# Norms of both graph layers tile by tile on VectorE, two residual products inside the attention loop, and the first expert block's tokens fetched ahead of the block table

## The reference, cut to what matters

```
h0  = layernorm(x)
h   = gat(h0; W1, 4 heads x 256) + b1          # layer 1, 1024 columns
h   = relu(layer_norm(h) * g1 + be1) + (h0 @ Wr1 + br1)
h1  = h
h   = gat(h1; W2, 1 head x 768) + b2           # layer 2
h   = layer_norm(h) * g2 + be2 + (h1 @ Wr2 + br2)
x   = x + h
y   = layernorm(x)                             # then the block's own norm, twice in a row
y   = y + causal_attention(norm(y))            # 12 heads
sel = argmax(norm(y) @ Wg)                     # one expert for each token
x   = x + y + relu(norm(y) @ W1[sel] + b1) @ W2[sel] + b2
```

## Time and profile before

| | us |
|---|---|
| median of 3 runs | 1133.53 (1133.08 to 1135.2) |
| the profiled execution | 1131.86 |
| its span, first to last instruction | 1129.8 |
| TensorE busy in it | 1042.2 (92%) |
| VectorE busy | 747.1 (66%) |
| ScalarE busy | 561.1 (50%) |
| GpSimd busy | 192.2 (17%) |

### The profile page before, as it was taken

One profiled execution on the slowest core, in us unless ns is written; L12 is line 12 of the kernel. 1 busy time (PEld: TensorE's weight loads), 2 busy tenths in 40 slices (PEclk: granted clock), 3 DMA queues, 4 the chain that ended last, 5 costly groups with the idle time before them and its releaser, 6 DMA issues.

```text
span 1129.8 us, 19057 instructions
## 1 busy us (share of the span) xinstructions
PE 1042.2 (92%) x6176; PEld 651.9 (58%) x6177; DVE 747.1 (66%) x1327; ACT 561.1 (50%) x744; POOL 192.2 (17%) x182
## 2 busy tenths in 40 slices
PE   5999888998999799989989399999999999999997
PEld 3555557745776576566768245555555555555554
DVE  6667768796665674259976598941118898989511
ACT  2667655702250253158853377731117777877311
POOL 2000000075205531045001111100101120301000
PEclk9999999999999899989999599999999999999999
DMA  8300030003507400030014599960007999999200
GB/s 307 101 0 0 1 112 1 1 18 133 127 1 152 84 1 1 1 108 2 3 60 130 174 384 332 387 237 18 24 0 258 384 358 372 372 369 383 96 17 3
DMA packets 92263, 155.60 MB, mean 138 GB/s; under 512 B 36507, under 2 KB 36587, under 8 KB 92214
## 3 DMA queue, kind: packets, MB, share of 16 engines
q1 hardware_dynamic: 89814, 149.20, 38.4%
q0 software_dynamic: 2400, 5.77, 1.4%
HBM read 153.21 MB, written 7.77 MB: 142 GB/s over the span
## 4 chain that ended last, share of the span: by engine, by line
PE 74%; DVE 13%; issue 5%; DMA 3%; ACT 2%; POOL 1%; DVEq 1%; SPq 0%; ACTq 0%; POOLq 0%
PE psum L1433 31%; PE psum L1669 17%; PE psum L1644 15%; DMA low<-in_L_ffn_W_dram 2%; PE psum L1421 2%; DVE area L1302 2%; PE psum L1471 2%; PE psum L1653 2%; PE psum L1565 1%; DVE smalls L975 1%; DVE area L987 1%; PE psum L1640 1%; DVE area L1057 1%; DVE area L1273 1%; DVE area L1134 1%
## 5 line engine op out<-in xcount | busy, mean ns | idle before, releaser
L1302 DVE TENSOR_TENSOR area<-low,area 128x1536 f16<-128x1536 f32 x144 | 245.8, 1754 | 14.0 <-ACT area L924 13.8
L1433 PE MATMUL psum<-area,low 128*125 128x512 f16 (+4 forms) x1116 | 245.9, 381 | 5.8 <-DVE low L1155 3.2
L1644 PE MATMUL psum<-area,low 128*128 128x512 f16 x972 | 220.4, 381 | 0.0
L924 ACT ACTIVATE area<-low 128x1536 f16<-128x1536 f32 x138 | 200.6, 1484 | 37.1 <-DMA low<-in_L_ffn_W_dram 30.8
L1669 PE MATMUL psum<-area,low 128*128 128x384 f16 x1296 | 219.0, 327 | 0.0
L1433 PE MATMUL psum<-area 125*128 125x64 f16 (+10 forms) x1452 | 195.8, 289 | 8.2 <-DVE area L1273 4.8
L1433 PEld LDWEIGHTS psum<-area,low 128*125 128x125 f16 (+2 forms) x1116 | 143.2, 141 | 101.6 <-issue 59.2
L1669 PEld LDWEIGHTS psum<-area,low 128*128 128x128 f16 x1296 | 127.1, 98 | 80.6 <-issue 1.3
L1433 PEld LDWEIGHTS psum<-area 125*128 125x128 f16 (+3 forms) x1452 | 126.9, 122 | 60.3 <-DVE area L1273 12.2
L1644 PEld LDWEIGHTS psum<-area,low 128*128 128x128 f16 x972 | 95.3, 98 | 113.6 <-issue 2.5
L935 ACT ACTIVATE low<-psum 128x512 f32<-128x512 f32 x54 | 31.9, 591 | 158.4 <-PE psum L1644 152.0
(11 more groups left out here) (226 smaller groups left out, 1205.4 us busy)
## 6 DMA issues: line engine op xcount, KB each, us to landing
low<-in_L_ffn_W_dram SPq DMA_DIRECT2D x144, 768.0 KB, 8.3
area<-in_L_gnn_W_dram SPq DMA_DIRECT2D x2, 3072.0 KB, 12.0
area<-in_L_gnn_Wr_dram SPq DMA_DIRECT2D x2, 3072.0 KB, 15.6
low<-in_x_dram SPq DMA_DIRECT2D x10, 336.0 KB
area<-in_L_ffn_Wv_dram SPq DMA_DIRECT2D x6, 384.0 KB, 6.2
area<-in_L_ffn_Wq_dram SPq DMA_DIRECT2D x6, 384.0 KB, 7.2
area<-in_L_ffn_Wk_dram SPq DMA_DIRECT2D x6, 384.0 KB, 6.5
area<-in_L_ffn_Wp_dram SPq DMA_DIRECT2D x2, 1152.0 KB, 6.7
```

The costliest lines, as they stand in the source:

```text
L924: act.activation(unit_parts(u)[0], raw_view(u), ACT.Copy).then_inc(high_ok, 1)
L1302: dve.tensor_tensor(low_, raw_view(u), high_, ALU.subtract).then_inc(low_ok, 1)
L1433: ins = pe.matmul(place(name)[0:parts, at:at + w], left(q), right(q)[:, at:at + w], start=(q == 0), stop=(q == k - 1))
L1644: ins = pe.matmul(psum[:, (c % 2) * BANK:(c % 2 + 1) * BANK], ht[x_][:, k, :], w1_s[c][w_][:, k, :], start=False, stop=(k == KD - 1 and x_ ...
```

## The change

*Layer 1.* The norm starts inside the loop's last head. Behind the evacuation of tile t (`behind1`) VectorE takes its statistics, then `centred` computes (row - mean) * g1 in one pass, and `shifted1` of the tile before computes rstd * row + be1. GpSimd keeps only the inverse roots, one per tile. The residual products of tiles 1 and 2 are taken as four halves of 512 columns at TensorE's steps 8, 15, 17 and 19, copied out of PSUM by ScalarE; tiles 3 and 4 stay behind the loop. VectorE's order there: residual rows 0 to 2, low half of W2, joins 0 to 2, then row and join of tiles 3 and 4.

*Layer 2.* The tile is centred and scaled by g2 in `behind2`; the factor rstd goes into the pass that adds it to the sum. GpSimd adds be2+br2 to x (`shift_x`), and each tile's load of x has a semaphore of its own. `residual_sum(0)` lies behind the statistics of tile 3, `first_norm_twice(0)` and `residual_sum(1)` behind those of tile 4.

*Routing.* Block 0 always belongs to expert 0, so its tokens follow from the ranks alone: an own item `ids0`, made before the block table; GpSimd fetches from it directly; ScalarE applies scale and shift for this block. TensorE turns these tokens before it makes `ids`.

```diff
+RES1_HALVES = {8: (1, 0), 15: (1, 1), 17: (2, 0), 19: (2, 1)}
...
+            def centred(rows_, t, g):
+                dve.wait_ge(var_ok, norms[0])
+                return dve.scalar_tensor_tensor(out=rows_[:, t, :], in0=rows_[:, t, :], scalar=mv[:, t, 0:1], in1=g,
+                                                op0=ALU.subtract, op1=ALU.mult)
...
-            graph_attention(1, HEADS, HID, agg1, row1["b1"])
-            variance(agg1, HC)
-            for t in range(T):
-                normal(agg1[:, t, :], agg1[:, t, :], t).then_inc(epi_a, 1)
+            def shifted1(t):
+                dve.wait_ge(rstd_ok, rows_normed + t + 1)
+                return dve.scalar_tensor_tensor(out=agg1[:, t, :], in0=agg1[:, t, :], scalar=rstd[:, t:t + 1],
+                                                in1=row1["be1"], op0=ALU.mult, op1=ALU.add)
+            def behind1(t):
+                was_emptied(dve, ("agg", 1, (HEADS - 1) * T + t))
+                moments(agg1, HC, t, t + 1)
+                centred(agg1, t, row1["g1"]).then_inc(epi_a, 1)
+                if t >= 1:
+                    dve.wait_ge(epi_a, t)
+                    shifted1(t - 1).then_inc(epi_b, 1)
+            graph_attention(1, HEADS, HID, agg1, row1["b1"], behind1)
+            dve.wait_ge(epi_a, T)
+            shifted1(T - 1).then_inc(epi_b, 1)
...
+            for t in range(3):
+                residual_row(t)
+            graph_low(1, w2_parts)
+            for t in range(3):
+                join_residual(t)
+            for t in range(3, T):
+                residual_row(t)
+                join_residual(t)
...
+                    if layer == 1 and i in RES1_HALVES:
+                        by_x0_half(*RES1_HALVES[i])
...
+            def behind2(t):
+                was_emptied(dve, ("agg", 2, t))
+                moments(agg2, D, t, t + 1)
+                centred(agg2, t, row2["g2"]).then_inc(epi_a, 1)
+                if t == T - 2:
+                    residual_sum(0)
+                if t == T - 1:
+                    first_norm_twice(0)
+                    residual_sum(1)
...
+            def shift_x(t):
+                pool.wait_ge(x2_in[t], 32)
+                pool.tensor_tensor(total[:, t, :], total[:, t, :], row2["be2"], ALU.add).then_inc(epi_b, 1)
+            for t in range(T):
+                if t == T - 1:
+                    inverse_root_twice(0)
+                inverse_root(t, t + 1)
+                if 1 <= t <= 3:
+                    shift_x(t - 1)
+            inverse_root_twice(1)
+            for t in range(3, T):
+                shift_x(t)
+            for t in range(2, T):
+                inverse_root_twice(t)
...
+            link(dve.tensor_tensor(spot0, cum[:, 0:T, 0], far, ALU.add))
+            for t in range(T):
+                ins = dve.tensor_scalar(row_hot0[:, t, :], iota128, spot0[:, t:t + 1], None, ALU.is_equal)
+            ins.then_inc(spots0_ok, 1)
...
+            done(dve, ("ids0",))
+            ins = dve.tensor_scalar(ids_first, place(("ids0",), 1), float(NOWHERE), None, ALU.add)
...
+            pool.wait_ge(ids0_ok, 1)
+            pool.indirect_dma_start(xt, None, n2_dram, bass.IndirectOffsetOnAxis(ap=ids_first, axis=0),
+                                    bounds_check=N - 1, oob_is_err=False).then_inc(xt_in, 16)
```

More of the change, by code:

```diff
@@ L71, in item_plan @@
             plan.append((("gate", t - 3), "A"))
-    plan += [(("rank",), "D"), (("ids",), "D")]
+    plan += [(("rank",), "D"), (("ids0",), "D"), (("ids",), "D")]
     return plan
@@ L169, in gnn_moe_kernel @@
         res1 = v3(A(4, 0, T * HC, P), T)
-        res1_early = low[0:P, TW + 4 * N:TW + 4 * N + HC]
-        assert 4 * N + HC <= XW
+        res1_early = [low[0:P, TW + 4 * N:TW + 4 * N + HC], T_[0:P, KD * N:KD * N + HC], A(0, KH * D // 2, HC, P)]
+        assert 4 * N + HC <= XW and KD * N + HC <= TW
         row_a2 = [A(2, 4096, D, P), A(2, 4096 + D, D, P)]
@@ L696, in _ @@
             pool.wait_ge(ht_ok, 1)
-            fetch_tokens(ids_all[:, 2:3], 2)
+            fetch_tokens(ids_all[:, 2:3], 1)
             with pool.Fori(0, blocks) as b:
@@ L814, in _ @@
                     if layer == 1 and i == 2:
-                        copy(("res1", 0), res1_early, place(("res1", 0), HC, P))
+                        copy(("res1", 0), res1_early[0], place(("res1", 0), HC, P))
+                    if layer == 1 and i - 2 in RES1_HALVES:
+                        t, q = RES1_HALVES[i - 2]
+                        copy(("res1", t, q), res1_early[t][:, q * BANK:(q + 1) * BANK], place(("res1", t, q), BANK, P))
                     if layer == 2 and i == 2:
@@ L910, in _ @@
                 early_high(u)
+            act.wait_ge(xt_used, 1)
+            for k in range(KD):
+                ins = act.activation(turned[:, k, :], psum[:, 6 * BANK + k * BR:6 * BANK + (k + 1) * BR],
+                                     ACT.Identity, scale=cols[:, 2, k:k + 1], bias=cols[:, 3, k:k + 1])
+            ins.then_inc(turned_ok, 1)
+            act.wait_ge(turned_ok, 1)
+            act.activation(ht[0], turned, ACT.Copy).then_inc(hthi_ok, 1)
             act.wait_ge(routed, 1)
@@ L1120, in graph_attention @@
                             scalar=rinv[:, q], in1=bias_row[:, h * width:(h + 1) * width], op0=ALU.mult, op1=ALU.add))
-                        if behind:
+                        if behind and h == heads - 1:
                             behind(t)
@@ L1207, in residual_norm, with first_norm_twice @@
                     was_emptied(dve, ("res2", t))
-                dve.wait_ge(epi_b, T + t + 1)
-                link(dve.tensor_tensor(total[:, t, :], agg2[:, t, :], total[:, t, :], ALU.add))
-                variance(total, D, t, t + 1)
+                dve.wait_ge(epi_a, T + t + 1)
+                dve.wait_ge(rstd_ok, first_norm + t + 1 + (t == T - 1))
+                link(dve.scalar_tensor_tensor(out=total[:, t, :], in0=agg2[:, t, :], scalar=rstd[:, t:t + 1],
+                                              in1=total[:, t, :], op0=ALU.mult, op1=ALU.add))
+                moments(total, D, t, t + 1)
+                roots[t] = norms[0]
+            def first_norm_twice(t):
+                dve.wait_ge(rstd_ok, roots[t])
                 if t >= 4:
@@ L1325, in _ @@
             dve.tensor_tensor(sel, sel, by_token(tmx), ALU.is_equal).then_inc(sel_ok, 1)
+            dve.wait_ge(sel_ok, 2)
+            link(dve.tensor_scalar(far, sel[:, :, 0], -2.0 * NOWHERE, 2.0 * NOWHERE, ALU.mult, ALU.add))
             done(dve, ("rank",))
@@ L1507, in _ @@
             graph_attention(1, HEADS, HID, xl1, lambda: by_x0(0, BANK))
-            for t in range(1, T):
+            for t in range(3, T):
                 by_x0(t)
@@ L1608, in _, with turn_tokens @@
             ins.then_inc(made, 1)
+            free(pe, ("ids0",))
+            pe.wait_ge(spots0_ok, 1)
+            for t in range(T):
+                ins = pe.matmul(place(("ids0",), 1), row_hot0[:, t, :], id16[:, t:t + 1], start=(t == 0), stop=(t == T - 1))
+            ins.then_inc(made, 1)
+            def turn_tokens(b):
+                pe.wait_ge(xt_in, b * 16 + 16)
+                for k in range(KD):
+                    ins = pe.transpose(psum[:, 6 * BANK + k * BR:6 * BANK + (k + 1) * BR],
+                                       xt[:, k * 128:(k + 1) * 128], ident)
+                ins.then_inc(xt_used, 1)
+            turn_tokens(0)
             free(pe, ("ids",))
```

113 lines of the change are left out of this document (48 added, 65 removed).

## The result

The changed kernel takes **1122.66 us** in the median of 4 runs (1118.5 to 1123.92) against 1134.28 of the kernel before on the same chip (4 runs): ratio **0.989, 95% interval 0.987 to 0.992**. The prediction was 1123.8, in the range 1115 to 1131. The execution that was profiled took 1123.52 us, span 1121.6; the one of before took 1131.86, span 1129.8, and the sum of the prediction, made against it, gave 1122.2. The brackets behind them are 95% intervals.

What follows compares the result with a forecast made beforehand. TensorE and VectorE nearly full in layer 1's loop, TensorE idle 8.2 us after layer 2's, small steps chained in routing. From 1131.86, +2.3 - 9.0 - 3.0 = -9.7 gives 1122.2; with 1.67 for the median, 1123.8, range 1115 to 1131.

Steps and rivals of the forecast that it cites:

- (b): Layer 2's norms: TensorE's idle time between layer 2's loop and the transformer part goes, -9.0 us.
- (c): Routing: block 0's tokens and the block table come earlier, so the expert weight loads start earlier, -3.0 us.
- (a): Layer 1's loop, with norm and halves moved in: layer-2 products start later, +2.3 us.
- The end of the VectorE chain: Layer 1: VectorE's work ahead of the layer-2 products ends at 272.1, against their start at 270.03 before.
- The clock term: Before layer 2's first product: 0.2 us added for a TensorE wait of some 6 us, where the clock may drop.
- n1(0): Layer 2, norm of tile 0: ready at 370.7, 1.5 us before TensorE ends its residual product at 372.2.
- gap of 8.2: TensorE's idle time between layer 2's loop and the transformer part, 372.2 to 380.4: claimed to go entirely, -8.2 us.
- The delay through POOL's queue: Layer 2: shifts of x(3) and x(4) ahead of the roots of tiles 2 to 4 on POOL, costing 0.9 us.
- (1): Rival: VectorE bounds layer 1's last head, its two-input passes taking 2.17 us instead of 1.22; total 1139, chance 0.08.
- (2): Rival, layer 2: n1(0) comes after TensorE's end, 5 us less gained; total 1129, chance 0.12.
- (3): Rival, routing: table and register loads are last and (c) brings nothing; total 1127, chance 0.12.
- (4): Rival, layer 1: halves fill idle time counted as unfillable, (a) gains 4 us; total 1117.5, chance 0.10.

Runs made afterwards that it cites:

- e1: Kernel before with only layer 1's part of the change: 1131.70 us, ratio 1.0017 to the kernel before.
- e3: Kernel before with only the routing part of the change: 1128.62 us, ratio 0.9980 to the kernel before.
- e8: Changed kernel with 18 extra matmuls, result overwritten, in TensorE's wait ahead of layer 2: 1117.48 us, ratio 0.9862 to the kernel before.
- e7: Changed kernel with POOL's shifts of x moved earlier, into layer 2's loop: 1118.51 us, ratio 0.9871 to the kernel before.
- e12: e9 with 8 extra matmuls, result overwritten, in the wait before the first layer-2 product: 1114.08 us, ratio 0.9827 to the kernel before.
- e2: Kernel before with only layer 2's part of the change: 1123.16 us, ratio 0.9925 to the kernel before.
- e11: Changed kernel with layer 1 as before the change: 1119.40 us, ratio 0.9864 to the kernel before.
- e5: Changed kernel with the first low part of h1T put ahead of the joins of tiles 3 and 4: 1118.95 us, ratio 0.9882 to the kernel before.
- e6: Changed kernel with only tile 1's halves in the loop, at steps 17 and 19, tile 2's product behind it: 1115.38 us, ratio 0.9847 to the kernel before.
- e9: Changed kernel with the edits of e6 and e7 together: 1115.44 us, ratio 0.9856 to the kernel before.
- e10: e9 with no halves in layer 1's loop, the norm still in the last head: 1122.52 us, ratio 0.9921 to the kernel before.

## Why the prediction was right, step by step

**The order of sizes was right**: (b) brings nearly all, (c) some 3, (a) costs a little. Forecast +2.3, -9.0, -3.0; measured +2.9, -8.5, -3.4, and in the profiles of the parts alone +2.6, -8.5, -3.1 (e1 to e3). The total came closer than the method can promise: 1122.66 for 1123.8, while executions of the changed kernel alone span 5.4 us, and the group of 108 matmuls added 1.7 to the profiled one that no term covers. For that execution the sum gave 1122.2 and it took 1123.52. That both numbers miss by so little, in opposite directions, is in part luck.

**(a), the halves in the loop.** The delay of the turn was put at 3.7 and is (193.54 + 0.65) - 190.49 = 3.70; that of product 15 at 8.7 and is 8.2. Two sums of the prediction don't come out of its own terms: with the loop's end at 242.8 for 223.7 not 17.6 but 19.1 us come back in the loop (measured 18.1), and W2's low part ends 11 us later than 251.1 by its terms, not 10 (measured 10.0). Neither enters the forecast. Steps of 4.0 us per tile in the last head hold, with 1.28 instead of 1.22 per pass. **The end of the VectorE chain** was put at 272.1 and came at 269.79 + 0.65 = 270.4, 1.7 early: 0.95 of it lies ahead of the end of the last shift (250.10 against a forecast of 251.7 less 0.65; its wait is 0.56, not 0.8), 0.75 behind it. So the delay put at 2.1 was 0.4. **The clock term was mis-sized**: 0.2 us for "some 6 us" of wait, measured 2.5, and 2.2 to 2.5 in four of four profiles with that wait; the granted clock and e8 show that it is the clock. The two errors, -1.7 and +2.3, nearly cancel, so the sum of (a) is right by luck and looks better than its terms. The mechanism was named but its price had no row behind it; the row of 381.68, 9.33 for 48 matmuls behind 8.22 us of idling, already said 1.3 at least.

**(b).** n1(0) was forecast for 370.7 and was ready at 371.07 with everything ahead of it 2.47 us later (the product of tile 2 starts at 366.66 for 364.19), so 2.1 early. The 1.8 that I charged for POOL's shift of x(2) fell on the other side: VectorE was first, and it was the shift at 365.11 that took 2.32, where those of x(0) and x(1) took 1.8. The gap of 8.2 is gone as forecast; turn and product behind it give 2.04, forecast 1.7, though its own rows held 2.0 (9.33 for 8.0 and 1.51 for 0.81); by the same terms its bound was -9.9 and not -10.1. The delay through POOL's queue was forecast at 0.9 and cost 1.7, by another route than I gave: not the roots queued behind the shifts, but the shifts beside VectorE's passes, and a PSUM slot emptied late. e7 shows it.

**(c).** That the table would be last and not the tokens is what happened. With the 4.49 us of the stages in front added back, the tokens' DMA starts at 633.4 (forecast 632.7 to 633.4), the tokens are on TensorE at 636.4 (636.0 to 636.7), the table is done at 641.2 (641.3 to 642.1) and the low tokens at 643.0 (643.4). The register load was 0.90 (I took 0.5). TensorE's own start, 639.76, is 2.2 us behind the low tokens' begin, where it was 1.3 before, with 6.16 us of idling put down to issue. That isn't on the chain that ended last: there the units of VectorE behind the low tokens are followed by a load of weights, at 645.24 for 653.11, 7.87 earlier like VectorE.

**The rivals.** (1) VectorE's passes at 2.17: they took 1.28. (2) n1(0) too late: 3.4 us early. (3) table and loads eat (c): the loads cost 0.4 more than forecast, and (c) still gave 3.4. (4) halves that fill idle time for nothing: those at 17 and 19 mostly do (2.65 for 10.3), those at 8 and 15 cost 8.3 for 10.3, and then make TensorE wait. I had priced the four as one set; apart, the two pairs point in opposite directions. Of the 6.4 us that e12 gains over the changed kernel up to the 504 matmuls, 2.2 come from leaving the first pair out, 2.5 from the clock and 1.8 from the shifts.

## What to carry to other kernels

Price each place to which work is moved by itself: here two halves (10.3 us) cost 2.65 us of loop where the partner engine had just been given more to do, and 8.3 where both were nearly full. Where a change lengthens a wait of TensorE, charge the stretch behind it with the slow product that the profile shows behind the nearest wait as long, take that as a chance and not as a certainty, and ask whether useless matmuls can lie in the wait. Set places in two traces against a common point near them, not against the start of the span. Of an elementwise pass on POOL ask what VectorE does beside it: the same shifts, queued one or two tiles earlier, cost nothing that the profile shows (e7).

## What the runs showed of the hardware

**Behind the same wait of TensorE its clock falls in some executions and not in others.** The first layer-2 product is 48 matmuls in each kernel. Behind the wait of 5.96 us it took 10.52, 10.20, 10.42 and 10.29. Behind 3.24 to 3.25 it took 8.02 (before), 8.01 (e2), 8.02 (e3), but 10.85 (e11). Behind 3.69 it took 9.70 (e5), behind 1.98 once 8.02 (e6) and twice 9.70 (e9, e10). With the wait filled to 0.70 and 0.25 it took 8.01 both times (e8, e12). In all six profiles with 8.01 to 8.02 the granted clock is 1.00 from the wait to the product's end; in the eight others it is 0.50 in a part of that stretch. In the changed kernel it falls at about 268, still in the wait; in e9 it is 1.00 up to the product's first us and 0.50 from 270 to 273, when TensorE is already busy again. The DMA traffic beside the wait doesn't decide it: the DMA engines were busy for a share of 0.99 in the changed kernel's, with 10.52, and as fully in e8's, with 8.01, but 0.03 in e9's, with 9.70. The Trainium skill warns of long idle gaps between matmul bursts (TensorE: Matmul & The Clock Gate, "Why this matters for your kernels"); here the clock fell behind gaps of 2 us too, in two profiles of three. The group of 108 matmuls behind its wait (2.57 us; 2.11 in e3, 2.33 in e5 and e6) took 17.73 or 17.74 in seven of the kernels' profiles, 19.22 to 19.42 in six, 20.73 in e12, with the same code; in e3, e5 and e6 the slow stretch also took in the turns in front (5.05 to 5.08 us for 30 of them, 3.59 in e1 and e7). These two places differ by up to 2.8 and 3.0 us, enough for the spread of the runs of one kernel (1118.5 to 1123.92 for the changed one), though only profiled executions show it. What decides in one execution is left open.

**A pass with one SBUF tensor isn't safe beside POOL.** The 768-column TENSOR_SCALAR took 0.68 alone and 2.07 and 2.16 beside POOL's TENSOR_TENSOR (e7 took it away), and 2.08 in the kernel before. In the other direction POOL's one-column roots beside VectorE's two-input passes went from 0.22 to 1.05 (L589) and from 0.57 to 1.13 (L590); the 1.05 is as long as the VectorE pass of 1.02 that began 0.05 us before it, at 362.83. In layer 1's last head L589 takes 1.31 beside passes of 1.28. Timeline of POOL in the changed kernel:

```profile
362.88 1.05 POOL L589 TENSOR_SCALAR smalls<-smalls 125x1 f32<-125x1 f32 x1 [3.52 <-DVE smalls L1002]
364.01 1.13 POOL L590 TENSOR_TENSOR smalls<-smalls 125x1 f32<-125x1 f32 x1
...
370.32 0.22 POOL L589 TENSOR_SCALAR smalls<-smalls 125x1 f32<-125x1 f32 x1
```
